# Spreading a fused attention kernel's side work differently over its 96 units: value blocks, second-branch projections and the last exponential

## The reference, cut to what matters

```python
qkv = xn @ Wqkv                                   # 256 -> q1,k1,q2,k2 (128 each), v (256)
# 16 heads of 8 values for q and k, 16 for v
A1 = causal_softmax(q1 @ k1.T / sqrt(8)) @ v      # first branch
A2 = causal_softmax(q2 @ k2.T / sqrt(8)) @ v      # second branch
diff = A1 - lam * A2                              # lam from four short vectors
diff = (1 - LAMBDA_INIT) * diff / sqrt(mean(diff**2) + eps)   # by head
attn = diff @ Wproj
ffn = (gelu(fp8(xn) @ g0) * (fp8(xn) @ g1)) as fp8 @ w_linear   # hidden 1024
out = x + attn + ffn
```

## Time and profile before

| what | value |
|---|---|
| median of 3 runs | 185.56 us (185.2 to 185.72) |
| the profiled execution's own time | 185.81 us |
| its span | 184.1 us, 4290 instructions |
| busy: TensorE, ScalarE | 177.2 us (96%), 163.2 us (89%) |
| busy: VectorE, GpSimd | 90.9 us (49%), 63.5 us (35%) |
| chain that ended last: ScalarE, TensorE | 77%, 18% |

### The profile page before, as it was taken

One profiled execution on the slowest core, in us unless ns is written; L12 is line 12 of the kernel. 1 busy time (PEld: TensorE's weight loads), 2 busy tenths in 40 slices (PEclk: granted clock), 3 DMA queues, 4 the chain that ended last, 5 costly groups with the idle time before them and its releaser, 6 DMA issues.

```text
span 184.1 us, 4290 instructions
## 1 busy us (share of the span) xinstructions
PE 177.2 (96%) x1810; PEld 77.3 (42%) x1810; DVE 90.9 (49%) x216; ACT 163.2 (89%) x145; POOL 63.5 (35%) x81
## 2 busy tenths in 40 slices
PE   6899999999999999999999999999999999989992
PEld 6787344443332423243334424334524434433381
DVE  2485879432313150440365022616551789979872
ACT  0678587999999999999999999999999999999810
POOL 8319950051207321450523053307403560323000
PEclk9999999999999999999999999999999999999999
DMA  5987658874000000000087876000000000000015
GB/s 170 382 307 226 164 144 193 213 166 108 0 0 5 0 0 4 0 0 4 15 204 171 207 164 166 0 0 4 4 0 0 4 0 4 0 0 4 0 57 178
DMA packets 8935, 15.02 MB, mean 82 GB/s; under 512 B 2000, under 2 KB 5584, under 8 KB 8912
## 3 DMA queue, kind: packets, MB, share of 16 engines
q1 hardware_dynamic: 8080, 13.92, 27.8%
q10 hardware_dynamic: 832, 0.79, 1.3%
HBM read 5.26 MB, written 1.05 MB: 34 GB/s over the span
## 4 chain that ended last, share of the span: by engine, by line
ACT 77%; PE 18%; DVE 2%; DMA 1%; issue 1%; ACTq 0%
ACT probs L493 74%; PE ps L958 7%; PE ps L1081 4%; PE ps L902 3%; PE ps L892 2%; DMA x_sb<-L_attn_x 1%; PE ps L882 1%; DVE parts L616 1%; ACT L455 1%; ACT L417 1%; PE ps L1050 1%; ACT parts L436 1%; PE ps L1038 0%; DVE stats L578 0%; PE ps L925 0%
## 5 line engine op out<-in xcount | busy, mean ns | idle before, releaser
L493 ACT ACTIVATE probs<-ps,shift 128x1536 f32<-128x1536 f32 x96 | 138.0, 1599 | 0.2 <-PE ps L1038 0.2
L1050 PE MATMUL ps<-probs,v_all 128*32 128x512 f32 (+3 forms) x768 | 78.3, 496 | 1.1 <-DVE o_t L709 0.8
L393 POOL TENSOR_SCALAR_AFFINE_SELECT probs<-probs 128x1024 f32<-128x1024 f32 (+1 forms) x40 | 36.7, 918 | 94.8 <-ACT probs L493 94.8
L1038 PE MATMUL ps<-q_st,k_st 32*128 32x512 f32 (+3 forms) x384 | 48.4, 411 | 0.0
L1038 PEld LDWEIGHTS ps<-q_st,k_st 32*128 32x128 f32 x384 | 22.5, 182 | 61.5 <-ACT probs L493 43.4
L709 DVE STREAM_TRANSPOSE o_t<-ps 128x512 f32<-128x512 f32 x16 | 11.5, 717 | 45.3 <-PE ps L1050 45.2
L1050 PEld LDWEIGHTS ps<-probs,v_all 128*32 128x32 f32 x768 | 16.2, 108 | 18.8 <-issue 9.5
L958 PE MATMUL ps<-area 128*128 128x512 fp8e4 x64 | 14.4, 379 | 0.2 <-DVE parts L616 0.2
L472 ACT ACTIVATE probs<-ps 128x512 bf16<-128x512 f32 x16 | 9.6, 597 | 3.5 <-PE ps L958 2.9
L634 DVE TENSOR_TENSOR area<-ps,probs 128x512 fp8e4<-128x512 f32 x16 | 10.9, 685 | 1.9 <-ACT probs L472 1.8
L355 POOL TENSOR_TENSOR squares<-parts 128x512 bf16<-128x512 f32 x8 | 8.7, 1099 | 2.1 <-DVE parts L773 2.1
(11 more groups left out here) (88 smaller groups left out, 128.0 us busy)
## 6 DMA issues: line engine op xcount, KB each, us to landing
q_st<-parts SPq DMA_DIRECT2D x32, 128.0 KB, 2.7
k_st<-parts SPq DMA_DIRECT2D x32, 128.0 KB, 2.8
probs<-L_ffn_w_gating SPq DMA_DIRECT2D x4, 512.0 KB, 7.3
probs<-L_ffn_w_linear SPq DMA_DIRECT2D x1, 1024.0 KB, 12.7
out<-probs SPq DMA_DIRECT2D x3, 256.0 KB, 2.3
x_sb<-L_attn_x ACTq DMA_DIRECT2D x2, 256.0 KB, 5.0
w_q<-L_attn_Wqkv SPq DMA_DIRECT2D x1, 512.0 KB, 9.1
w_q<-L_attn_Wqkv SPq DMA_DIRECT2D x1, 256.0 KB, 3.8
```

Of the source, the lines that this page charges most:

```text
L393: pool.affine_select(out=blocks, in_=blocks, pattern=pattern, compare_op=ALU.is_ge, fill=0.0, base=0, channel_multiplier=-1).then_inc(mask ...
L493: act.activation(probs[:, at:at + PER_UNIT, :].rearrange("p s u -> p (s u)"), ps[:, 3 * (n % 2):3 * (n % 2) + 3, :].rearrange("p b n -> p ...
L1038: ins = pe.matmul(ps[:, bank, at:at + wide * P], k_st[rows, g % STACKS, kb * P:(kb + 1) * P], q_st[rows, g % STACKS, queries], start=True, ...
L1050: ins = pe.matmul(ps[32 * j:32 * j + 32, 6, q0 % HALF:q0 % HALF + wide * P], v_all[:, g % HG, kb, 32 * j:32 * j + 32], probs[:, slot + j, ...
```

## The change

It moves side work between units and changes a few orders:

- one block of values is projected a unit from unit 0 (blocks 1 to 6 in units 0 to 5), and the last block 7 in two halves in units 8 and 9; VectorE copies it behind `take(0, 0)`;
- the second branch's projections end in unit 41 instead of 37, the norm product is in unit 44 instead of 41, the down projection is in units 45 to 83 instead of 44 to 79, and what follows (`REST_AT`, `Y_AT`) is at 87 and 90, 91. The places of `split`, `down`, `square_of` and `residual` on VectorE and GpSimd follow;
- ScalarE runs a dummy square root at the start, its dummy gelu one step earlier, and the last transposed block is copied by VectorE instead;
- the last exponential is two instructions of 256 columns of each item, and the last value product follows it by halves; the last scaling and transposing is by two times eight blocks;
- one warm-up matmul fewer. The exponential is written with a three-dimensional pattern instead of a flat one.

```diff
-WARM_UP, KEEP_UP = 11, 3
+WARM_UP, KEEP_UP = 10, 3
...
-V_AT = {0: (1, 2), 1: (3,), 2: (4,), 3: (5,), 4: (6,), 5: (7,)}
-QK_AT = {8: (4, 0, 0, 256), 9: (4, 0, 256, 256), 13: (4, 1, 0, 512), 17: (5, 0, 0, 512), 20: (5, 1, 0, 256),
-         21: (5, 1, 256, 256), 25: (6, 0, 0, 512), 29: (6, 1, 0, 512), 32: (7, 0, 0, 256), 33: (7, 0, 256, 256),
-         37: (7, 1, 0, 512)}
-NORM_AT = 41
-DOWN_AT = {44: (0, 0, 4), 45: (0, 4, 8), 49: (1, 0, 8), 53: (2, 0, 8), 56: (3, 0, 4), 57: (3, 4, 8), 64: (4, 0, 8),
-           67: (5, 0, 4), 68: (5, 4, 8), 75: (6, 0, 8), 78: (7, 0, 4), 79: (7, 4, 8)}
-
-REST_AT, Y_AT = 83, 87
+V_AT = {0: (1,), 1: (2,), 2: (3,), 3: (4,), 4: (5,), 5: (6,)}
+
+LAST_V_AT = (8, 9)
+QK_AT = {13: (4, 0, 0, 512), 17: (4, 1, 0, 512), 20: (5, 0, 0, 256), 21: (5, 0, 256, 256), 25: (5, 1, 0, 512),
+         29: (6, 0, 0, 512), 32: (6, 1, 0, 256), 33: (6, 1, 256, 256), 37: (7, 0, 0, 512), 41: (7, 1, 0, 512)}
+NORM_AT = 44
+DOWN_AT = {45: (0, 0, 4), 49: (0, 4, 8), 53: (1, 0, 8), 56: (2, 0, 4), 57: (2, 4, 8), 64: (3, 0, 8), 67: (4, 0, 4),
+           68: (4, 4, 8), 75: (5, 0, 8), 78: (6, 0, 4), 79: (6, 4, 8), 83: (7, 0, 8)}
+
+REST_AT, Y_AT = 87, (90, 91)
...
-                    if (g, c) in ((1, 2), (1, 5), (2, 5), (3, 0)):
-                        square_of(4 + ((1, 2), (1, 5), (2, 5), (3, 0)).index((g, c)))
-                    if (g, c) in ((4, 4), (5, 2), (6, 0), (6, 5)):
-                        residual(((4, 4), (5, 2), (6, 0), (6, 5)).index((g, c)))
+                    if (g, c) in ((1, 4), (2, 1), (3, 0), (3, 4)):
+                        square_of(4 + ((1, 4), (2, 1), (3, 0), (3, 4)).index((g, c)))
+                    if (g, c) in ((4, 5), (5, 4), (6, 5), (7, 2)):
+                        residual(((4, 5), (5, 4), (6, 5), (7, 2)).index((g, c)))
...
             act.wait_ge(eps_set, 1)
+            act.activation(lam_w[:, 7:8], eps[:, 0:1], ACT.Sqrt)
...
             upper(0)
-            turned(3)
+
+            act.activation(lam_w[:, 6:7], rstd[:, 1, 0:1], ACT.Gelu_apprx_tanh)
             upper(1)
-
-            act.activation(lam_w[:, 6:7], rstd[:, 1, 0:1], ACT.Gelu_apprx_tanh)
...
+                for e in range(1 if n < UNITS - 1 else 2):
+                    cols = slice(e * C, (e + 1) * C) if n == UNITS - 1 else slice(0, HALF)
+                    act.activation(probs[:, at:at + PER_UNIT, cols], ps[:, 3 * (n % 2):3 * (n % 2) + 3, cols],
...
             x_to_fp8(0)
             rest(0, QK_BANK[0])
+            turned(3)
+            rest(1, QK_BANK[1])
             x_to_fp8(1)
-            rest(1, QK_BANK[1])
...
-            for b in range(0, TB, 2):
+            for b in range(0, TB - 2, 2):
                 values_in(b)
+            values_in(TB - 2, (0,))
...
-            keep(0, 0)
+            take(0, 0)
+            values_in(TB - 2, (1,))
+            divide(0, 0)
+            keep(0, 1)
             split(4)
-            keep(0, 1)
...
+            keep(2, 0)
             split(6)
-            keep(2, 0)
+            keep(2, 1)
             split(7)
-            keep(2, 1)
             bound1 = Bound(dve, own, 1)
...
             with dve.If(large2 == 0):
+                keep(3, 1)
                 down(0)
-                keep(3, 1)
...
-            scale_by_root(3, last)
-            turn_back(1, 1)
+            for b in (16, 24):
+                scale_by_root(3, slice(b, b + 8))
+                turn_back(1, b, 8)
...
+                if (g, c) == (GROUPS - 1, NC - 1):
+                    product(g, c, 0, kb, 2, q0, False)
+                    pe.wait_ge(exp_done, UNITS + 1)
+                    product(g, c, 2 * P, kb, 2, q0 + 2 * P, False).then_inc(o_ready, 1)
+                    return
...
                 pe.wait_ge(out_t_ready, 4)
                 project(4, 1)
-                for b in (5, 6, 7):
+                project(5, 1).then_inc(y_ready, 1)
+                pe.wait_ge(out_t_ready, 5)
+                for b in (6, 7):
                     project(b, 1).then_inc(y_ready, 1)
```

More of the change, by code:

```diff
@@ L492, in _ @@
                 act.wait_ge(scores_ready, n + 1)
[L493 to L496, removed]
+                for e in range(1 if n < UNITS - 1 else 2):
+                    cols = slice(e * C, (e + 1) * C) if n == UNITS - 1 else slice(0, HALF)
+                    act.activation(probs[:, at:at + PER_UNIT, cols], ps[:, 3 * (n % 2):3 * (n % 2) + 3, cols],
+                                   ACT.Exp, bias=shift[:, br, 1, hg * BR + br:hg * BR + br + 1], scale=SCALE
+                                   ).then_inc(exp_done, 1)
             def whole(b):
@@ L610, in _, with turned @@
             even_block(3)
+            def turned(i):
+                dve.wait_ge(xt_ready, i + 1)
+                dve.tensor_copy(xn_t[:, :, i * C:(i + 1) * C], ps[:, i, :].rearrange("p (k n) -> p k n", k=KC)
+                                ).then_inc(xt_out, 1)
             def rest(u, bank):
@@ L754, in scale_by_root, with turn_back, values_in @@
                                            root[:, s].unsqueeze(2).broadcast_to([P, n, DV]), ALU.mult))
-            def turn_back(p, h):
-                dve.transpose(out_t[:, p, h * HALF:(h + 1) * HALF],
-                              fin[:, 16 * h:16 * h + 16, 2 * p:2 * p + 2, :].rearrange("p b g d -> p b (g d)")
+            def turn_back(p, first, n):
+                dve.transpose(out_t[:, p, 32 * first:32 * (first + n)],
+                              fin[:, first:first + n, 2 * p:2 * p + 2, :].rearrange("p b g d -> p b (g d)")
                               ).then_inc(out_t_ready, 1)
-            def values_in(b):
-                dve.wait_ge(v_ready, b // 2 + 1)
-                for e in range(2):
+            def values_in(b, blocks=(0, 1)):
+                dve.wait_ge(v_ready, b // 2 + 1 + (b == TB - 2 and blocks == (1,)))
+                for e in blocks:
                     dve.tensor_copy(v_all[:, :, b + e, :].rearrange("p g (j w) -> p g j w", j=J)[:, :, :, 0:DV],
@@ L819, in _ @@
             with dve.If(large2 == 0):
+                keep(3, 1)
                 down(0)
-                keep(3, 1)
             all_of, first, last = slice(0, 32), slice(0, 16), slice(16, 32)
             take(4, 0)
-            down(1)
             own.step(difference(0, 0))
@@ L828, in _ @@
             take(4, 1)
+            down(1)
             own.step(difference(0, 1))
@@ L831, in _ @@
             take(5, 0)
-            down(2)
             own.step(difference(1, 0))
@@ L835, in _ @@
             take(5, 1)
+            down(2)
             differ(1, 1)
@@ L839, in _ @@
             mean_of(1, 1)
-            down(3)
             inverse_root(slice(0, 64))
@@ L843, in _ @@
             scale_by_root(1, all_of)
-            turn_back(0, 0)
-            turn_back(0, 1)
+            turn_back(0, 0, 16)
+            turn_back(0, 16, 16)
             own.step(difference(2, 0))
             mean_of(2, 0)
+            down(3)
             take(6, 1)
@@ L856, in _ @@
             scale_by_root(2, all_of)
-            turn_back(1, 0)
+            turn_back(1, 0, 16)
             take(7, 1)
@@ L904, in queries_keys, with project_values @@
                                  skip_group_check=True)
-            def project_values(b):
+            def project_values(b, only=None):
                 if b == 0:
                     pe.wait_ge(wv_in, 16)
-                for k in range(KC):
+                for k in range(KC) if only is None else (only,):
                     ins = by_quarters(V_BANK[b // 2], b % 2 * C, xn_t[:, k, b * P:(b + 1) * P], w_q[:, k, 2 * C:3 * C],
                                       k == 0, k == KC - 1)
-                if b % 2 == 1:
+                if (b % 2 == 1 or b == TB - 2) and only != 0:
                     ins.then_inc(v_ready, 1)
@@ L967, in beside @@
                     project_values(b)
+                if n in LAST_V_AT:
+                    if n == LAST_V_AT[0]:
+                        pe.wait_ge(v_out, TB - 1)
+                    project_values(TB - 1, LAST_V_AT.index(n))
                 if n in QK_AT:
@@ L1060, in values @@
                 (kb, wide, q0), *more = CHUNKS[c]
+                if (g, c) == (GROUPS - 1, NC - 1):
[3 more added lines that the diff above has]
+                    return
                 if g == 0 and c == 0:
                     pe.wait_ge(v_out, 6)
+                elif g == 0 and c == 5:
+                    pe.wait_ge(v_out, TB)
                 if c == 0 and g > 0:
@@ L1075, in second_half @@
                 pe.wait_ge(o_taken, 2 * g + 1)
+                if g == 0:
+                    pe.wait_ge(v_out, kb + 1)
                 product(g, MIXED, first[1] * P, kb, wide, q0, True)
@@ L1117, in attention @@
                         residual(1)
-                    if n == Y_AT:
+                    if n in Y_AT:
                         pe.wait_ge(wp_in, 16 * 8)
                         pe.wait_ge(out_t_ready, 2)
-                        project(0, 0)
-                        project(1, 0)
```

(1 more changed line is left out.)

## The result

The change made the kernel slower: 189.91 us median of 4 runs (189.8 to 190.92) against 185.45 of before (4 runs); ratio 1.0251, 95% interval 1.0223 to 1.028. The profiled execution took 189.80 us with a span of 188.1; before it was 185.81 and 184.1. The forecast was 187.5, in a range of 186.3 to 189.7: the direction is right, but the forecast loss of 1.9 us is less than half of the 4.5 us measured, and 189.91 lies just outside the range.

A forecast was written before the change was run, and what follows sets the result against it. It took ScalarE's run of exponentials as the bound, with TensorE nearly as busy. Terms -1.03 - 0.33 - 0.40 + 3.9 - 0.2 = +1.94 on 185.81 gave 187.75, forecast as 187.5 us median; range 186.3 to 189.7.

The forecast's parts named there:

- head: Before the first exponential: earlier table loads and one warm-up matmul fewer give -1.03 us, bounds -0.7 and -1.3.
- unit 1, small losses: Main stretch: unit 1's wait for scores goes, -0.33 us; TensorE's lead covers small losses, -0.40, bounds 0 and -0.40.
- wait for take(3, 0): Units 45 and 46: second rectangle waits for take(3, 0) behind Bound, exponentials stand still 3.9 us, bounds 3.0 and 4.4.
- clock behind the wait: TensorE's clock after unit 45's wait: no term in the sum; only rival (a) priced a fall, 1.5 to 3.1 us.
- ending: After the last exponential: TensorE's chain sets the end, halving is worth little, -0.2 us, bounds 0 and -0.7.
- The step that decides: Norm product in unit 44: Bound starts at 98.15, take(3, 0) follows at 101.63, unit 46's exponential is late, +3.9 us.
- stack 4: Its last DMA lands at 102.6, covered by 3.7 us for unit 48; without the stall, about 0.9 at most.
- rival (a): TensorE's clock drops to 1.2 GHz around the wait, 1.5 to 3.1 us more: 189.0 to 190.6; chance 0.16.
- the prediction's own last line: The prediction is wrong if the gap at unit 46 is under 2 us, or if the clock falls.

The follow-up runs named there:

- head_only: The kernel before with only the head's edits (one warm-up matmul fewer, dummy square root, earlier dummy gelu, last transposed block on VectorE): 184.64 us, ratio 0.9949.
- keep_clock: The changed kernel with 14 dummy matmuls on TensorE in unit 45's wait for take(3, 0): 188.49 us, ratio 1.015 to the kernel before.
- before_norm44: The kernel before with only the norm product moved from unit 41 to 44, first down projection put together in unit 45: 191.17 us, ratio 1.0311.
- take_first: The changed kernel with take(3, 0) moved ahead of Bound on VectorE, its divide left behind: 185.15 us, ratio 0.9974 to the kernel before.
- norm_43: The changed kernel with the norm product in unit 43 instead of 44, last square behind mask (3, 2): 190.51 us, ratio 1.0255 to the kernel before.
- q_early: take_first with the four query DMAs of stack 4 issued once the query projections are split: 184.83 us, ratio 0.9954 to the kernel before.

## Why the prediction was right and wrong

Of the 4.0 us between the two profiled executions, by its terms:

| term | forecast | profile | by runs |
|---|---|---|---|
| head | -1.03 | -1.27 | -0.95 (head_only) |
| unit 1, small losses | -0.33 - 0.40 | -0.33 - 0.27 | |
| wait for take(3, 0) | +3.9 | +3.85 (keep_clock) | |
| clock behind the wait | 0 | +1.55 | +1.9 |
| units 90 to 92 | 0 | +0.35 | |
| last exponential halved | 0 | +0.16 | |
| ending | -0.2 | -0.04 | |

**Right.** The step that decides was read from the old trace: `Bound` ahead of `take(3, 0)`, 3.48 us long, now behind the last square and the norm product. It came out as 3.85 us against 3.9, and the norm product began at 96.45 where the forecast has 97.70 less the head's 1.27; before_norm44 and take_first show it as the cause. Unit 1's wait went, TensorE's lead covered the small losses up to unit 45, and stack 4 was covered only while the stall was there: with the stall gone it cost 0.68, within the 0.9 I had given.

**Wrong.** The step that failed is the clock behind the wait. The sum has no term for it: in rival (a) a fall of the clock was worked out at 1.5 to 3.1 us and then given a chance of 0.16, though the stall itself was held for nearly certain. The runs show 1.55 us by the profiles and 1.9 by the runs of keep_clock. By the prediction's own last line it was wrong if the clock fell, and it did: all 4 runs of the changed kernel have a mean granted clock of 0.979 to 0.988, those of norm_43 and before_norm44 0.973 to 0.991, while keep_clock has 0.997 or more. The time of (a), 189.0 to 190.6, holds 189.91; the range's upper end cut through it. I had argued that a trace with TensorE busy 96% says nothing on a long wait. That left the chance open; it did not make it small. By the rule that I cited (the Trainium skill, TensorE: Matmul & The Clock Gate, "HAM oscillation") the rival was to be the forecast, and the trace agrees with it: idle from 97.3 to 101.1, half clock behind.

The price in (a) rests on a reading of the head: that TensorE began at 1.2 GHz and rose inside the transposes. The view of the granted clock reads 1.00 from the start in both kernels, so it doesn't show this. The lengths of the records speak for it: the warm-up's 22 take 5.06 us, 0.23 each, and keep_clock's 28 of the same form take 3.39, 0.12 each, at a grant of 1.00.

Smaller terms failed near the end. The sum had nothing for the output projections in units 90 and 91, which cost 0.35 where TensorE's lead of some 0.24 ran out, nor for the halved exponential, which cost 0.16. And the -0.2 for the ending was not there (-0.04): the lead that was to give it had been spent in those two units.

The head's total is right partly by luck. The first projection started at 7.31 instead of 8.80, 1.49 earlier, where 0.83 was forecast. But the third hidden step started at 18.18, 1.27 earlier, and still waited 0.22 for a split of VectorE, where the forecast had no wait.

The page on table loads (the Trainium skill, ScalarE: Activation LUTs, "What ACT_TABLE_LOAD costs") has a drain of over a microsecond beside the load. Here the load of 1.28 at 2.27 is followed by its activation at 3.57, 0.02 behind its end: this trace shows no drain.

## What to carry to other kernels

When work is moved to a later place, ask what stands behind it on every engine that waits for it: here a norm product moved by three units held a PSUM bank through a chain of small VectorE instructions that had nothing to do with the bank. Release a shared buffer first, then compute. And when a forecast has TensorE idle for as long as here (3.3 to 3.9 us) in a stretch where it is the bound, put the half clock behind it into the sum, and compare a wait of nothing with one filled with dummy matmuls.

## What was not expected

- In the profiled executions a shorter wait had a longer slow stretch: 3.87 us of wait and 3.4 at half clock in the changed kernel, 3.27 and 6.8 in norm_43. In the first the grant fell just behind the wait, in the second at about 100.0, while TensorE was still idle. The runs of one kernel differ in it as well, and what decides between the two they don't show.
- Filling the wait with 14 dummy matmuls gave 1.4 us back by the medians (189.91 to 188.49), 1.9 by the ratios to the kernel before.
- take_first's 12 runs spread over 184.36 to 186.57, those of before over 185.33 to 185.99; q_early's six stay within 184.36 to 185.2. That the late stack makes the spread fits, but q_early was timed on another chip and half as often, so no run tells it.
- The issue of an output DMA took 0.37 to 0.39 us for one and 0.86 to 1.24 for another close behind it, whether from SyncE or ScalarE. What makes it slow the runs don't show.
